# Masked keys zeroed on GpSimd after the exp, and the next layer's tables scaled earlier

## What is computed

```
dot = einsum('bqhd,bkhd->bhqk', q, k)
dot = where(causal, dot, -inf)                    # later keys get no weight
attn = softmax(dot, axis=-1)
out = einsum('bhqk,bkhd->bqhd', attn, v)
...
q = l2norm(q) * qs                                # qs, ksc: one vector of 64 for each layer
k = l2norm(k) * ksc
q = q * cos * scale + rotate_half(q) * sin * scale
k = k * cos / scale + rotate_half(k) * sin / scale
```

## Time and profile before

| | |
|---|---|
| median of 3 runs | 4537.34 us (4535.16 to 4538.42) |
| the profiled execution | 4535.16 us, of which the span is 4533.5 us |
| busy share of the span | PE 87%, DVE 65%, ACT 45%, POOL 16% |
| mean granted TensorE clock | 0.925 |
| instructions | 61872 |

### The profile page before, as it was taken

The page is one execution under the profiler, slowest core; times in us unless marked ns, Lnnn a source line. Parts: engine busy times, 40 slices in busy tenths (PEclk is TensorE's granted clock), DMA queues, the critical chain, the costliest instruction groups (busy, mean ns, idle before and its releaser), DMA issues. The chain is left out here.

```text
span 4533.5 us, 61872 instructions
## 1 busy us (share of the span) xinstructions
PE 3958.7 (87%) x21496; PEld 1939.8 (43%) x21588; DVE 2967.0 (65%) x5867; ACT 2043.3 (45%) x3711; POOL 717.8 (16%) x566
## 2 busy tenths in 40 slices
PE   7898977899979988898949899679899799879987
PEld 6233344233335555454523333443333455545544
DVE  3887766888757742675259786759786677337743
ACT  2365642365645531554124566324566455215531
POOL 2100004000023312331130000040000233123311
PEclk8799988799989999999978999888999899989999
DMA  3212002212010001000031110021110100110000
GB/s 80 37 19 38 3 2 47 31 23 35 1 59 5 1 10 56 12 1 7 9 75 29 29 29 1 2 50 28 30 29 2 59 6 1 36 37 5 1 10 23
DMA packets 127150, 108.97 MB, mean 24 GB/s; under 512 B 38473, under 2 KB 119921, under 8 KB 125809
## 3 DMA queue, kind: packets, MB, share of 16 engines
q1 hardware_dynamic: 126832, 104.92, 11.4%
HBM read 41.15 MB, written 4.19 MB: 10 GB/s over the span
## 5 line engine op out<-in xcount | busy, mean ns | idle before, releaser
L745 DVE TENSOR_REDUCE chunk_max<-banks 128x1 f32<-128x512 f32 (+3 forms) x2240 | 1403.1, 669 | 220.8 <-PE banks L637 138.1
L712 ACT ACTIVATE probs<-banks 128x1024 f32<-128x1024 f32 (+3 forms) x1280 | 1084.2, 894 | 867.6 <-PE banks L681 434.9
L634 PE MATMUL banks<-stack_k,stack_q 96*128 96x512 bf16 (+3 forms) x2560 | 846.7, 378 | 137.1 <-DMA stack_k<-parts 56.4
L677 PE MATMUL banks<-stack_q,stack_k 99*128 99x512 bf16 (+3 forms) x2560 | 701.5, 351 | 7.4 <-ACT probs L712 7.4
L653 PE MATMUL banks<-probs,values_group 128*17 128x512 f32 (+3 forms) x5120 | 594.5, 536 | 0.0
L634 PEld LDWEIGHTS banks<-stack_k,stack_q 96*128 96x128 bf16 x2560 | 248.2, 100 | 790.1 <-DVE chunk_max L745 502.8
L1305 ACT ACTIVATE probs_l<-banks,nmax 128x256 f32<-128x256 f32 x512 | 238.2, 470 | 474.8 <-DVE nmax L1422 474.8
L1179 PE MATMUL banks<-wqkv,hT 128*128 128x512 f32 x768 | 362.9, 611 | 2.4 <-issue 2.4
L1549 PE MATMUL banks<-hnT,w 128*128 128x512 f32 x768 | 341.3, 605 | 3.5 <-ACT hnT L1572 3.5
L1361 POOL TENSOR_TENSOR inv_norm<-ssum,mhalf 128x8 f32<-128x8 f32 x128 | 210.8, 1647 | 750.3 <-DVE ssum L1393 744.0
L677 PEld LDWEIGHTS banks<-stack_q,stack_k 99*128 99x128 bf16 x2560 | 241.3, 99 | 204.0 <-ACT probs L712 58.5
(11 more groups left out here) (183 smaller groups left out, 5102.8 us busy)
## 6 DMA issues: line engine op xcount, KB each, us to landing
stack_q<-parts SPq DMA_DIRECT2D x384, 64.0 KB, 2.4
stack_k<-parts SPq DMA_DIRECT2D x384, 64.0 KB, 2.4
xpos<-in_c_xpos SPq DMA_DIRECT2D x4, 2048.0 KB, 8.3
wqkv<-in_L_ffn_wqkv SPq DMA_DIRECT2D x12, 512.0 KB, 12.3
w<-in_L_ffn_w SPq DMA_DIRECT2D x16, 341.0 KB, 4.1
x_tok<-in_L_attn_x SPq DMA_DIRECT2D x8, 512.0 KB, 6.0
rope<-in_c_rope SPq DMA_DIRECT2D x2, 2048.0 KB, 7.7
hs_f<-x_mid SPq DMA_DIRECT2D x16, 256.0 KB
```

The lines of the kernel that those rows point to most:

```text
L634: ins = pe.matmul(out, sq[0:KS, c, j0 + j, i * P:(i + 1) * P], sk[0:KS, cc, j0 + j, 0:width], start=True, stop=not diag, skip_group_check= ...
L677: ins = pe.matmul(ps[:, SCORE + j, off:CH], keys, sq[0:KS + PARTS, c, j, off:CH], start=True, stop=not diag, skip_group_check=True)
L712: act.activation(probs[:, s % 2, 2 * half:2 * half + 2, off:CH], ps[:, SCORE + 2 * half:SCORE + 2 * half + 2, off:CH], ACT.Exp)\
L745: dve.tensor_reduce(chunk_max[:, n % 2, j:j + heads, i, cc], bank[:, 0:heads * width].rearrange("p (h n) -> p h n", h=heads), AX.X, ALU.ma ...
```

## The change

Two edits that do not touch each other. In `attend` the mask matmuls of the second pass (L681) go away. GpSimd instead sets the weights of later keys to zero in `probs`, in the 128 columns of the diagonal for four heads in one `affine_select` of 128 x 512 elements; it waits for both halves of the exps, and `pv` of a diagonal step waits for it. The first pass keeps its masks (L637), so the maxima are those of the allowed keys. In `feed_forward` of layer 0, the loads of the next local layer are issued by SP right behind the row load of chunk 1 and no longer behind that of chunk 3, and POOL scales the tables after the bias adds of chunk 1 and no longer after those of chunk 3.

```diff
+DIAGONAL = [s for s, (n, g, c, kt) in enumerate(STEPS) if kt >= TPC * c]
...
             @block.gpsimd
             def _(pool):
                 pool.memset(stacks[1][1][KS:KS + PARTS, :, :, :], 1.0).then_inc(S["ones_rows"], 1)
+                pool.wait_ge(S["ones_rows"], 1)
+                for i, s in enumerate(DIAGONAL):
+                    off = (STEPS[s][3] - TPC * STEPS[s][2]) * P
+                    pool.wait_ge(S["exped"], 2 * s + 4)
+                    pool.wait_ge(S["causal"], i)
+                    block = probs[:, s % 2, :, off:off + P]
+                    pool.affine_select(block, block, [[0, GH], [1, P]], ALU.is_ge, 0.0, base=0, channel_multiplier=-1)\
+                        .then_inc(S["causal"], 1)
...
                     pe.wait_ge(S["exped"], 2 * s + 4)
+                    if s in DIAGONAL:
+                        pe.wait_ge(S["causal"], DIAGONAL.index(s) + 1)
...
                         ins = pe.matmul(ps[:, SCORE + j, off:CH], keys,
-                                        sq[0:KS + PARTS, c, j, off:CH], start=True, stop=not diag,
+                                        sq[0:KS + PARTS, c, j, off:CH], start=True, stop=True,
                                         skip_group_check=True)
-                        if diag:
-                            ins = pe.matmul(ps[:, SCORE + j, off:off + P], identb[:, :], k["mask_kq"][:, :],
-                                            start=False, stop=True, skip_group_check=True)
...
                 for c in range(1, NCH):
                     sp.wait_ge(S["normed"], TPC * c)
                     load_shifted(sp, hs, x2, c, early["h_in"])
-                if l + 1 < DEPTH:
-                    load_local_weights(k, sp, l + 1)
+                    if c == 1 and l + 1 < DEPTH:
+                        load_local_weights(k, sp, l + 1)
...
                         pool.tensor_tensor(xt, xt, b2[:, :], ALU.add)\
                             .then_inc(S["x_out"], 1)
+                    if c == 1 and l + 1 < DEPTH:
+                        build_tables(k, pool)
...
                 loop(emit)(pool)
-                if l + 1 < DEPTH:
-                    build_tables(k, pool)
```

More of the change, by code:

```diff
@@ L568, in attend @@
               + " ".join(f"rows{n}" for n in range(len(ITEMS)))
-              + " ones_rows scored bank_read max_out max_split scores_kq exped pv_done cleared o_out values_in recip w_in")
+              + " causal ones_rows scored bank_read max_out max_split scores_kq exped pv_done cleared o_out values_in recip w_in")
     SCORE, PV, FIRST_PASS, NFP = 0, 4, 5, 3
@@ L662, in _ @@
                     off = max(0, kt - TPC * c) * P
-                    diag = kt >= TPC * c
                     slots = steps_slots(s)
```

## The result

| | median | lowest to highest | ratio to before |
|---|---|---|---|
| before | 4536.25 us | 4532.2 to 4538.42 | |
| after | 4487.62 us | 4485.86 to 4491.79 | 0.9895 [0.9883, 0.9908] |

The change makes the kernel 48.6 us faster. The profiled execution of after took 4491.79 us, the slowest of its four, and its span is 4490.4 us against 4533.5, so 43.1 us less. Two of the runs of before further down, 4634.77 and 9864.73 us, were disturbed executions and are in no comparison.

A forecast was written before the change was run, and what follows sets the result against it. PE bounds attention, with DVE close behind in early items; POOL's tables alone end layer 0's feed-forward. Attention +9.0 and tables -18.4 give -9.4 us: 4537.34 to 4528 us, range 4502 to 4592.

The forecast's parts named there:

- d: Duration of one 128 x 512 select on POOL in attention's diagonal steps, taken as 1.1 us.
- The formula: Change of the whole kernel in us: 40d - 64.8, plus 44(d - 0.84) where d is over 0.84.
- the cheap select: Rival on the select in attention: d below 0.95; at 0.92 the sum is -24.5 us; chance 0.25.
- the forecast's case: Select in attention with d from 0.95 to 1.2: change of -22 to -1 us; chance 0.30.
- the dear one: Rival in attention: d above 1.2 and PE waits in pv; +4.9 us at 1.27, +45 at 1.75; chance 0.40.
- the early items: First 11 items of each attention, 44 in all: mask removal gains 0.7 us each; shortest gap without masks 1.04, at d2.
- the late items: Items 11 to 15 of each attention, 20 in all: mask removal gains 0.57 us; net change each 2L - 1.32.
- The rivals of another price for the masks: Early items gain only 0.5 us or nothing: forecast rises 9 or 31 us; chance inside the select cases.
- the gaps of 0.48 and 0.27: Late items, masks gone: PE's time in us between end of exps and their pv, at d0 and d2.
- the 0.57 of a late item: Attention's items 11 to 15: us kept from removing the masks in each, of a ceiling of 0.96.
- L = d + 0.2: Diagonal steps in attention: the select's result comes L us after the exps end; 1.3 at d = 1.1.
- The cover: Layer 0 feed-forward, chunk 2: 3.3 us of POOL lateness hidden before DVE's normalise; each microsecond beyond is paid.

The follow-up runs named there:

- the kernel without selects: The changed kernel without the select and without PE's wait for it, second-pass masks also gone, so masking is left out; 4464.3 us, 0.9835.
- the shorter write: The changed kernel with one POOL write of 128 x 4096 elements to scratch behind chunk 2's tables; 4491.93 us, 0.9904.

## Why the prediction was wrong

**The size of d is the step that failed.** "A select reads one operand and writes, as the copy does, and computes an index and a comparison for each element. I take the middle between copy and two operands, d = 1.1": it measured 0.637 us, near the lower end, 0.60. The formula turned this into time faithfully: at 0.637 it gives -39.3 us in place of -9.4. The rival that came true is the cheap select, with 0.25 against 0.30 for the forecast's case and 0.40 for the dear one. What was argued against it, that the comparison comes on top, was no row: the only row for one operand was a copy of 256 elements at 0.458, and the select of 256 elements takes 0.406, less than that copy. The range began at d = 0.75, above the lower bound that the text itself had set; carried down to 0.60 it would have reached 4496 us, still 9 above the result.

**The rest of the miss** is 10 us in attention, and against it the 6 us between the stages. In attention it is -30.8 measured and -20.9 by the formula at 0.637 without the tables: the early items, -0.76 each in place of -0.70, -2.6; what item 5 gained beyond that in three attentions, -5.6; the late items with their ends, +8.3 in place of +9.9, -1.6. The rivals of another price for the masks fall with the kernel without selects: early items keep 0.80 of 0.96.

**Right, and shown**: the gaps of 0.48 and 0.27, the 0.57 of a late item, L = d + 0.2, payment at d0 and d2 only (the table above). Wrong was the early items' gap at d2: with the masks gone it is 0.84 in five of the eleven, 0.78 in two and 1.03 to 1.21 in the rest, not 1.04 at the least; and 1.21 was not the shortest before, two items had 1.15. At L = 0.85 this made almost no difference, while with the select twice it took the early items' gain nearly whole (0.15 left, item 5 aside); there four of them waited at d0 too, by 0.06 to 0.12.

**The tables**: -18.4 forecast, -18.3 in the traces, -19.7 in the medians. The cover, 3.3 us for DVE, is confirmed by the shorter write. That each microsecond beyond it is paid in full is not: 10.2 us of DVE's wait cost 7.6 by the medians, since PE had work for longer. SP's queue and the loads hid as forecast. DVE was not slowed beside the tables: its statistics of chunk 3 take 1.40 us both at 1733.64 in before, where POOL is idle, and at 1720.97 in after, where POOL scales the tables.

## What to carry to other kernels

Where one operation's duration decides the sign, its range should reach from bound to bound: this unmeasured one-operand operation came out near the cheapest row, and the range stopped short of it. A mask moved behind the exp costs its lateness only where the next engine has less slack than that; walking a late item from wait to wait gave these gaps to within 0.01 us, also for changes not yet made, while the early items, which were not walked, were missed by 0.20. Work on a helper engine that waits for two halves was worth cutting at the halves: 256 more instructions on POOL, and 14 us less. A change inside one stage can move the clock at the start of the next, here by about 1 us each time.

## What the runs showed of the hardware

GpSimd's `affine_select` of f32 took 0.637 us for 128 x 512 and 0.406 us for 128 x 256: about 0.90 ns for an element of a row and 0.18 us fixed. The former is half the price of a two-operand operation of that size, 1.267. A write of 16384 elements on the same engine took 13.75 us, 0.84 ns for each. From the end of ACT's exp to POOL's start passed 0.07 us, and from POOL's end to PE's waiting matmul 0.14.

The granted clock at a stage's start is not fixed by that stage's own code: 0.78 and 0.80 in two stretches of 4 us before, 0.56 and 0.59 after, 1.1 us of time, and over 8 us 0.79 behind all four attentions in two traces without the select, 0.57 in five with it.

What stays open: what in the select's waits delays the clock, 2.5 us that the stages between the attentions took longer, 1.0 to 1.7 us of item 5's gain in each of three attentions, and the wait of nearly 14 us for `stack_k` in each attention, which no run touched.
